# Routing in three phases inside the attention, second choices ranked from the top of an expert's rows, and another order of an attention's first steps

## What is computed

```python
probs = jax.nn.softmax(logits, axis=-1)
top1 = jnp.argmax(probs, axis=-1)
top2 = jnp.argmax(jnp.where(m1 > 0, -jnp.inf, logits), axis=-1)
loc1 = jnp.cumsum(m1, axis=0) - 1.0
loc2 = jnp.cumsum(m2, axis=0) - 1.0 + m1.sum(axis=0, keepdims=True)
m1 = m1 * (loc1 < C); m2 = m2 * (loc2 < C)
h = jax.nn.gelu(jnp.einsum('ecd,edf->ecf', xin, fc1_w) + fc1_b[:, None, :])
eout = jnp.einsum('ecf,efd->ecd', h, fc2_w) + fc2_b[:, None, :]
```

## Time and profile before

| | us |
|---|---|
| median of 3 runs (lowest, highest) | 2134.05 (2132.18, 2135.73) |
| the profiled execution | 2132.52 |
| its span, first to last instruction | 2130.4 |
| PE busy | 1588.8 |
| DVE busy | 1344.6 |
| POOL busy | 1074.2 |
| ACT busy | 944.5 |

### The profile page before, as it was taken

The page is one execution under the profiler, slowest core; times in us unless marked ns, Lnnn a source line. Parts: engine busy times, 40 slices in busy tenths (PEclk is TensorE's granted clock), DMA queues, the critical chain, the costliest instruction groups (busy, mean ns, idle before and its releaser), DMA issues. The chain is left out here.

```text
span 2130.4 us, 44441 instructions
## 1 busy us (share of the span) xinstructions
PE 1588.8 (75%) x16560; PEld 899.4 (42%) x16560; DVE 1344.6 (63%) x3121; ACT 944.5 (44%) x2000; POOL 1074.2 (50%) x1761
## 2 busy tenths in 40 slices
PE   3345888873459899972788389999999999826872
PEld 3242333332435555541334145555555555513431
DVE  8628877826298877738322488777777777473214
ACT  1112666641217567640222146666666666602221
POOL 2144757421438576420777347346456674305773
PEclk9985899965859999985888679999999999957996
DMA  6142223201423233300343333323233233002435
GB/s 207 39 138 79 82 82 84 80 22 40 139 82 112 70 95 92 87 17 25 82 90 93 99 102 91 86 78 99 77 85 92 82 103 86 28 25 61 97 81 145
DMA packets 227411, 178.66 MB, mean 84 GB/s; under 512 B 33479, under 2 KB 216143, under 8 KB 226816
## 3 DMA queue, kind: packets, MB, share of 16 engines
q1 hardware_dynamic: 211776, 155.26, 25.7%
q0 software_dynamic: 10240, 17.96, 4.2%
q10 hardware_dynamic: 5184, 2.63, 0.4%
HBM read 104.34 MB, written 72.35 MB: 83 GB/s over the span
## 5 line engine op out<-in xcount | busy, mean ns | idle before, releaser
L701 DVE TENSOR_REDUCE mx<-PS 128x2 f32<-128x512 f32 (+3 forms) x1408 | 780.5, 610 | 218.4 <-PE PS L386 166.6
L560 ACT ACTIVATE pt<-PS 128x512 f32<-128x512 f32 (+2 forms) x1408 | 657.9, 539 | 316.4 <-PE PS L386 241.2
L402 PE MATMUL PS<-ka,qa 52*128 52x256 bf16 (+3 forms) x2048 | 486.4, 308 | 57.1 <-DVE mx L701 47.4
L511 PE MATMUL PS<-qa,ka 55*128 55x512 bf16 (+3 forms) x1792 | 468.2, 320 | 34.9 <-DMA qa<-nm 28.4
L456 PE MATMUL PS<-pt,vs 128*32 128x512 f32 (+3 forms) x3584 | 348.7, 482 | 0.0
L1244 POOL DMA_INDIRECT pt<-xn_rows,idx x160 | 165.6, 1035 | 340.3 <-DVE idx L1179 292.8
L386 PE MATMUL PS<-mask_q,identh 64*128 64x64 bf16 x3072 | 316.3, 193 | 0.0
L386 PE MATMUL PS<-mask_k,identh 64*128 64x64 bf16 x3072 | 309.3, 190 | 0.0
L511 PEld LDWEIGHTS PS<-qa,ka 55*128 55x128 bf16 x1792 | 166.5, 94 | 262.4 <-issue 135.9
L386 PEld LDWEIGHTS PS<-mask_q,identh 64*128 64x128 bf16 x3072 | 260.6, 98 | 31.5 <-issue 7.8
L386 PEld LDWEIGHTS PS<-mask_k,identh 64*128 64x128 bf16 x3072 | 251.4, 96 | 47.9 <-issue 2.2
(11 more groups left out here) (223 smaller groups left out, 2287.0 us busy)
## 6 DMA issues: line engine op xcount, KB each, us to landing
pt<-in_f_w SPq DMA_DIRECT2D x96, 256.0 KB, 3.3
q_parts<-parts SPq DMA_DIRECT2D x192, 128.0 KB, 2.4
qa<-q_parts SPq DMA_DIRECT2D x256, 96.0 KB, 2.3
k_parts<-parts SPq DMA_DIRECT2D x144, 128.0 KB, 2.4
ka<-k_parts SPq DMA_DIRECT2D x192, 96.0 KB, 2.4
xn_rows<-xn SPq DMA_DIRECT2D x32, 256.0 KB, 2.4
xn<-y_rows SPq DMA_DIRECT2D x32, 256.0 KB, 4.7
hid<-y_rows SPq DMA_DIRECT2D x32, 256.0 KB, 5.3
```

Source lines behind the costliest of these rows:

```text
L402: mm = pe.matmul(PS[:, bank, i * n:(i + 1) * n], k.qa[rows, b % 2, g, h // 2, qb * P:(qb + 1) * P], k.ka[rows, b % 2, g, h // 2, 0:n], sta ...
L511: mm = pe.matmul(PS[:, bank, i * n:(i + 1) * n], k.ka[rows, b % 2, g, h // 2, kb * P:(kb + 1) * P], k.qa[rows, b % 2, g, h // 2, q0:S], st ...
L560: nc.scalar.activation(k.pt[:, u % 2, at[c]:at[c] + len(heads) * n], PS[:, SC_BANK + c % RING, 0:len(heads) * n], ACT.Exp, scale=SCORE_SCA ...
L701: nc.vector.tensor_reduce(out, PS[:, MX_BANK + t % RING, 0:len(heads) * n] .rearrange("p (h n) -> p h n", n=n), AX.X, ALU.max).then_inc(s. ...
```

## The change

**Routing.** `Routing`, `choose`, `ranks`, `mark`, `mark_high`, `occupants` and `index` take the place of the head of `moe`. The 32 tiles are routed in phases of 20, 8 and 4 tiles (`PHASES`); the very first routing is one phase of 32, in the front block. A phase's `choose` makes both one-hot tables (11 linked steps) and one running sum over all its columns; `ranks` is six matmuls of the phase's columns (and two or more short ones for the counts carried over); `mark` handles both choices in one pass. A second choice's rank is counted from the top end of its expert's rows, so that it doesn't need the total of first choices; the gates take that total in at the end. Phase 0 is chosen in unit U-2 and marked in unit U-1; phase 1 is chosen between `o_T` and `out` of the tail and marked after `front_rows`; phase 2 follows the last logits. Multiplying the high marks goes to POOL (`mark_high`), but for phase 2 of an attention.

**Experts.** What the gates need (`differences`, `shares`, `gates`) stands between the copies of the first experts, and the scaling of the source between those of experts 1 to 8. SP waits for the stores and loads the results of batch 0 before the block ends.

**Ramp.** `enter(2)` goes: POOL adds batches 2 (ahead of unit 0) to 7 (units 1, 2, 5, 6, 9), the DVE makes deviations at units 3, 7 and 11. `norm(1)` follows the key split and the values, and unit 0's maxima follow it at once; batch 1's projections stand between unit 1's maxima. The parts of a side go out in three DMAs, each repeating its source for 3, 2 and 1 rows, each as soon as its part is there. ACT loads the exponential's table first.

```diff
-WRITES = NPROD
+WRITES = 3
...
+class Routing:
...
+def choose(nc, k, chain, r, j):
...
+    over_e = lambda ap: ap.unsqueeze(2).to_broadcast([P, n, E])
+    logits, held, rest = e3(k.logits[:, cols]), e3(k.rw[:, 0:n * E]), e3(k.rw[:, 512:512 + n * E])
+    onehot = [r.onehot(k, j)[:, c].rearrange("p e t -> p t e") for c in range(2)]
+    for c, values in ((0, logits), (1, rest)):
+        top, last = k.rv[:, c, a:b], k.rv[:, 2 + c, a:b]
+        if c == 1:
+            chain.link(nc.vector.scalar_tensor_tensor(rest, onehot[0], MASKED, logits, ALU.mult, ALU.add))
+        chain.link(red(top, values, AX.X, ALU.max))
+        chain.link(tt(held, values, over_e(top), ALU.is_equal))
+        chain.link(tt(held, held, broadcast_rows(r.w.down, n), ALU.mult))
+        chain.link(red(last, held, AX.X, ALU.max))
+        chain.link(tt(onehot[c], held, over_e(last), ALU.is_equal))
+    upto, flat = r.upto(k, j), k.onehot[:, 2 * E * a:2 * E * b]
+    nc.vector.memset(upto[:, 0:1], 0.0)
+    chain.link(nc.vector.tensor_tensor_scan(upto[:, 1:], k.onesf[:, 0:1].to_broadcast([P, 2 * E * n]), flat, 0.0,
+                                            ALU.mult, ALU.add))
+    before, upto_end = r.ends(k, j)
+    ins = tt(k.carry[:, j, 0:2 * E], upto_end, before, ALU.subtract)
+    if 0 < j < len(r.phases) - 1:
+        chain.link(ins)
+        ins = tt(k.carry[:, j, 0:2 * E], k.carry[:, j, 0:2 * E], k.carry[:, j - 1, 0:2 * E], ALU.add)
+    ins.then_inc(s.choice_ready.h, 1)
+    chain.eng.wait_ge(*s.choice_ready.at(j + 1))
...
+def ranks(pe, k, r, j):
...
+    pe.wait_ge(*s.choice_ready.at(j + 1))
+    spread = lambda ap: ap.unsqueeze(2).to_broadcast([P, E, n])
+    by_e = lambda ap: ap.rearrange("p (e t) -> p e t", e=E)
+    before, upto, onehot = r.ends(k, j)[0], r.upto(k, j)[:, 1:], r.onehot(k, j)
+    for c in range(2):
+        out = PS[:, RANK_BANK + c, 0:n * E]
+        pe.matmul(out, k.onesb[:, :], upto[:, c * E * n:(c + 1) * E * n], start=True, stop=False)
+        pe.matmul(by_e(out), k.minus[:, :], spread(before[:, c * E:(c + 1) * E]), start=False, stop=False)
+        if j:
+            pe.matmul(by_e(out), k.onesb[:, :], spread(k.carry[:, j - 1, c * E:(c + 1) * E]), start=False, stop=False)
+        mm = pe.matmul(by_e(out), k.upper[:, :], onehot[:, c], start=False, stop=True)
+    if j == len(r.phases) - 1:
+        first = max(j - 1, 0)
+        for i in range(first, j + 1):
+            mm = pe.matmul(PS[:, RANK_BANK, 512 - E:512], k.onesb[:, :], k.carry[:, i, 0:E], start=(i == first), stop=(i == j))
+    mm.then_inc(s.rank_full.h, 1)
...
+def mark(nc, k, chain, r, j, alone):
...
+    rank, part, row, tile, last = both(10), both(12), both(14), both(16), both(2)
+    held = k.rw[:, 0:2 * n * E].rearrange("p (c e t) -> p c e t", c=2, e=E)
+    chain.eng.wait_ge(*s.rank_full.at(j + 1))
+    chain.link(tt(held, k.PS[:, RANK_BANK:RANK_BANK + 2, 0:n * E].rearrange("p c (e t) -> p c e t", e=E), r.onehot(k, j),
+                  ALU.mult))
+    chain.link(nc.vector.tensor_reduce(rank, held.rearrange("p c e t -> p c t e"), AX.X, ALU.add))
+    chain.link(nc.vector.tensor_scalar(part, rank, float(P), None, ALU.is_ge))
+    for m in range(2, ST):
+        chain.link(stt(part, rank, float(m * P), part, ALU.is_ge, ALU.add))
+    chain.link(stt(row, part, -float(P), rank, ALU.mult, ALU.add))
+    stt(tile[:, 0, :], last[:, 0, :], -float(ST), part[:, 0, :], ALU.mult, ALU.add)
+    chain.link(stt(tile[:, 1, :], last[:, 1, :], -float(ST), part[:, 1, :], ALU.mult, ALU.subtract))
+    marks = [r.marks(k, c, a, b) for c in range(2)]
+    for c, (low, high) in enumerate(marks):
+        last_high = tt(high, broadcast_rows(r.w.tile_names[c], n), tile[:, c, :].unsqueeze(2).to_broadcast([P, n, r.tiles]),
+                       ALU.is_equal)
+    chain.link(last_high)
+    for c, (low, high) in enumerate(marks):
+        last_low = nc.vector.tensor_scalar(low, high, k.lane[:, 0:1], None, ALU.mult)
+    if alone:
+        chain.link(last_low)
+        for c, (low, high) in enumerate(marks):
+            last_high = tt(high, high, k.row_high[:, a:b].unsqueeze(2).to_broadcast([P, n, r.tiles]), ALU.mult)
+        last_high.then_inc(s.high_ready.h, 1)
+    for c in range(2):
+        last_row = tt(k.at_rank[:, c, a * P:b * P].rearrange("p (t r) -> p t r", r=P), broadcast_rows(k.row_names[c], n),
+                      row[:, c, :].unsqueeze(2).to_broadcast([P, n, P]), ALU.is_equal)
+    last_row.then_inc(s.marks_ready.h, 1)
+    chain.eng.wait_ge(*s.marks_ready.at(j + 1))
...
+def occupants(pe, k, r, j):
+    s, (a, b) = k.sig, r.phases[j]
+    pe.wait_ge(*s.marks_ready.at(j + 1))
+    pe.wait_ge(*s.high_ready.at(j + 1))
+    for c in range(2):
+        for t in range(a, b):
+            mm = pe.matmul(k.PS[:, INV_BANK, c * 2 * r.tiles:(c + 1) * 2 * r.tiles], k.at_rank[:, c, t * P:(t + 1) * P],
+                           k.in_tile[c][:, 2 * r.tiles * t:2 * r.tiles * (t + 1)], start=(c == 0 and t == 0), stop=(c == 1 and t == NT - 1))
+    if j == len(r.phases) - 1:
+        mm.then_inc(s.inv_full.h, 1)
...
+def index(nc, k, chain, r):
...
+    chain.eng.wait_ge(*s.inv_full.at(1))
+    inv = k.PS[:, INV_BANK, 0:4 * n].rearrange("p (c a n) -> p c a n", c=2, a=2)
+    found = k.rw[:, 0:2 * n].rearrange("p (c n) -> p c n", c=2)
+    token, empty = k.rw[:, 512:512 + n], k.rw[:, 768:768 + n]
+    chain.link(nc.vector.tensor_copy(found, inv[:, :, 1, :]))
+    chain.link(nc.vector.tensor_tensor(found, inv[:, :, 0, :], found, ALU.add))
+    chain.link(stt(token, found[:, 0, :], 0.0, found[:, 1, :], ALU.is_equal, ALU.mult))
+    chain.link(nc.vector.tensor_tensor(token, token, found[:, 0, :], ALU.add))
+    ts(k.idx[:, 0, 0:n], token, -1.0, float(T), ALU.min, ALU.add)
+    chain.link(ts(empty, found[:, 0, :], 0.0, float(T), ALU.is_equal, ALU.mult))
+    stt(k.idx[:, 1, 0:n], empty, float(T), token, ALU.add, ALU.add).then_inc(s.idx_ready.h, 1)
+    chain.link(ts(k.before[:, 0:r.E], k.PS[:, RANK_BANK, 512 - r.E:512], float(r.w.counted), None, ALU.min))
 def front_counts(k):
...
+    LATE_ENTRY = {-1: 2, 1: 3, 2: 4, 5: 5, 6: 6, 9: 7}
+    LATE_ROOT = {3: 3, 7: 4, 11: 5}
     entered = lambda b: sum(first <= b for first, n in ENTRY_GROUPS)
...
         if u in LATE_ENTRY:
             events += [("late0", LATE_ENTRY[u])]
-        if u - 1 in LATE_ENTRY:
+        if u - 1 in LATE_ENTRY and u:
             events += [("late2", LATE_ENTRY[u - 1])]
-        if u == max(LATE_ENTRY) + 2:
-            events += [("late_root", 3)]
+        if u in LATE_ROOT:
+            events += [("late_root", LATE_ROOT[u])]
...
+        if u == U - 2:
+            events += [("choose", 0)]
+        if u == U - 1:
+            events += [("ranks", 0), ("mark", 0)]
...
+            for name in ENTRY + ("v",):
+                project(name, 0)
             pe.wait_ge(*s.steps_landed.at(32))
-            for u in range(2):
-                for t in range(NMX):
-                    max_tile(u, t)
-                if u == 0:
-                    max_transpose(u)
+            for t in range(NMX):
+                max_tile(0, t)
+            max_transpose(0)
+            for t in range(NMX):
+                max_tile(1, t)
+                if t in (2, 5):
+                    project(ENTRY[t // 3], 1)
...
-            for name in ("ctx_T", "out", "f_T", "f_l"):
+            for name in ("ctx_T", "out"):
                 tail(name, NB - 1)
+            ranks(pe, k, r, 1)
+            occupants(pe, k, r, 0)
+            for name in ("f_T", "f_l"):
+                tail(name, NB - 1)
+            occupants(pe, k, r, 1)
+            ranks(pe, k, r, 2)
+            occupants(pe, k, r, 2)
...
-                for name in ENTRY:
-                    copy(name, b)
+            nc.scalar.activation(k.spare[:, 0:1], k.ident[:, 0:1], ACT.Exp)
+            for name in ENTRY:
+                copy(name, 0)
             copy("nm", 0)
+            for name in ENTRY:
+                copy(name, 1)
             for u in range(U):
                 for name, n in order(u):
...
             split_first_keys()
             value_rows(0)
-            if conv:
-                convolve(1)
-            enter(2)
-            for u in range(2):
-                for t in range(NMX):
-                    max_tile(u, t)
+            norm(1)
+            for t in range(NMX):
+                max_tile(0, t)
+            for t in range(NMX):
+                max_tile(1, t)
+                if t == 5 and conv:
+                    convolve(1)
+            entry(2, 2)
+            entry_deviations(2)
...
+                    elif name == "choose":
+                        dve.wait_ge(*s.gl_free.at(PHASES[0][1] // TB))
+                        choose(nc, k, route, r, 0)
+                    elif name == "mark":
+                        dve.wait_ge(*s.pv_done.at(U - 1))
+                        mark(nc, k, route, r, 0, False)
             tail("o_T", U // 2 - 1)
+            dve.wait_ge(*s.gl_free.at(PHASES[1][1] // TB))
```

(55 more changed lines are left out.)

337 lines of the change are left out of this document (159 added, 178 removed).

## The result

The changed kernel takes 2060.35 us (median of 4 runs, 2055.78 to 2064.37) beside 2133.11 us before (4 runs, 2121.93 to 2135.73): a ratio of 0.967, 95% interval 0.963 to 0.971. The forecast was 2032 us, 2010 to 2058. The direction was right; 73 us came in place of 102, and the median lies 2 us above the range. The profiled execution has a span of 2059.4 us and a time of 2061.11.

What follows compares the result with a forecast made beforehand. It took linked DVE routing chains as the bound for 167 us, then ramp waits, with PE bounding units and POOL's DMAs experts. 8.6 + 16.6 + 44 - 5.7 + 32.5 + 2.4 + 4 = 102.4 us gave 2032 us, range 2010 to 2058.

Steps and rivals of the forecast that it cites:

- Routing in the attentions: Logits to first fetch inside attentions: phases partly hidden beside units, 16.6 us gained with 8 experts, 22 twice with 16.
- The rule on the running sum: DVE running sums in routing: built-in one goes at half throughput, by which the sums would cost 1.5 us more in all.
- First routing: One-phase routing of 8 experts in the front block: first fetch at 84.5 against 93.2, 8.6 us gained.
- the step that said it is hidden: choose(0) in unit U-2: 320 columns, 6.9 us, hidden because no row maxima are left there.
- the step that failed: Attention units: three smaller late_roots replace one that stops PE 4.8 us, and POOL adds one more batch; 4 us gained.
- The prediction's own first paragraph: What bounds the kernel: a linked DVE step costs 0.155 us plus columns/960, and 0.035 to the next.
- The bounds 0 and 9: Limits set on the gain in the attention units, in us, of which 4 was taken.
- Ramps: Attention's block start to first score: earlier result loads, split writes and maxima gain 32.5 us over three ramps.
- The keys' path: Last ramp: batch 0 as before until its keys at 1207.0, then key loads at 1217.8 against 1227.81.
- Experts: Expert stages: gates ahead of result(0) delays the first delivery and so all, 5.7 us lost together.
- the first (ramps give half): Rival: first score waits for something after the maxima, ramps give 16 in place of 32.5, 2048 us; chance 0.12.
- The second (POOL in full): Rival: tail handovers pay POOL's products in full, 5 us more per 16-expert tail, 4 in others, 2050; chance 0.12.

Runs made afterwards that it cites:

- The held `choose(0)`: Changed kernel with choose(0) held until POOL's front rows are written, ranks(0) and mark(0) later: unit U-2 18.4 and 16.9 us, last score to fetch 45.3 and 45.1.
- the high products on the DVE: Changed kernel with the high products of phases 0 and 1 on the DVE, none on POOL: last score to first fetch 43.5 and 43.8 us.
- the spread roots: Changed kernel with three late roots issued one step behind each maximum tile: second attention's body 330.3 us, 18.3 less, of which 3.0 are unit 0's.

## Why the prediction was right and wrong

*Routing in the attentions*: right in its mechanism. Forecast 16.6, 22 and 22; measured 18.8, 22.1 and 22.2 from the last score on (19.7, 19.0 and 21.3 if the last unit, which now holds `ranks(0)`, is counted in), with `o_T` 5.6 us later, `mark(0)` 13.1 (12.8). That the last two came to 0.2 is in part luck. Two sizes inside were too small: POOL beside `choose(1)` 3.2 instead of 2.5, and `choose(1)` on its own 5.7 instead of 4.5. The stretch from `out` to the logits made up for them: 7.9 us where 9.0 was measured before and 9.6 forecast. PE, busy there with `occupants`, was granted a higher clock (last column but two; the kernel before, then the changed one), and its transposes and gate products, 1.12 and 1.86 us before, took 0.66 and 1.24:

```profile
1869.60:1878.60 9.00, 2.98 (x12) 2.50 (x12) 4.36 (x21) 0.99 (x2) 0.00 (x0) 0.50 0.10 29
1833.20:1841.10 7.90, 6.49 (x60) 6.00 (x60) 7.28 (x31) 1.00 (x2) 0.00 (x0) 0.72 0.12 35
```

The 1.2 us in `choose(1)` are the two one-hot writes, 0.9, and the running sum, 0.3. In its strided bf16 order a one-hot write of 128 columns takes 0.72 us where f32 in row order takes 0.29. The Trainium skill has this in "SBUF — State Buffer", "Door 1: The DMA port swizzle", in its remark on cachelines: an access that goes to a new 16-byte line each time pays for it, and these elements lie eight bf16, 16 bytes, apart. The trace agrees. The same instruction with 64 columns, in phase 1 of the first attention (16 bytes apart) and in phase 2 of the last (8 bytes apart):

```profile
458.60 0.44 DVE L313 TENSOR_TENSOR onehot<-rw,rv 128x64 bf16<-128x64 f32 x1
1848.39 0.30 DVE L313 TENSOR_TENSOR onehot<-rw,rv 128x64 bf16<-128x64 f32 x1
```

The Trainium skill has two hits to a line as enough there for full speed; here two elements to a line still took longer than 64 f32 columns in row order, 0.22 us. Whether that is the stride or the bf16 output, no run tells. The rule on the running sum (cited in the prediction) holds: 256 columns took 0.69 us, where a product of 512 does.

*First routing*: 6.6 of 8.6. `mark` took 13.2 (13.3); `choose` took 8.3 and not 6.0, by the same strided writes and sums.

*`choose(0)` beside the units*: the step that said it is hidden, since the DVE idles, looked at one engine. It priced POOL beside the DVE in the tail and not here, where the DVE's steps stretch POOL's rows, for which PE waits: unit U-2 grew by 5.7 and 4.4 us, and 4.2 of each is this wait. It also took 6.9 us for a phase that measures 9.9. The held `choose(0)` removed the wait in unit U-2 and lost as much behind it, so no run shows a place for it that costs nothing.

*Units*: the step that failed, and with it the prediction. It read the earlier trace rows rightly (a root stops PE 4.8 us and makes its unit 7 longer) and then wrote that three smaller ones take its place for a gain of 4. The prediction's own first paragraph has the reason against it: a step costs a fixed part, and a root of 4 or 16 columns is all fixed part. By its steps alone three roots cost three times the one; measured, 26.0 us in three units against 7.0 in one, +19.0, as they also stand where POOL splits (6.9 us each, against 5.6 for the old one). Unit 0's +5.7 (+2.8 in the runs with the longer ramp) is the third batch's root, for which the prediction took 3 in the ramp. In all the units gave +37.6 where -4 was put, 41.6 us off: 24.7 of it are roots, 10.1 the two units U-2 with `choose(0)`. The bounds 0 and 9 were both on the side of gain, so no part of the range stood for units that grow. That the median missed the range by only 2 us is luck: the ramps' 13 us more than forecast hid part of the error.

*Ramps*: 45.5 instead of 32.5, a term mis-sized on the side of gain. In the last one the first sum came 5.1 us after the last delivery, before the change 12.7 (1200.55 in the earlier trace rows less 1187.9); the forecast had 7.2 from the block's start against 9.1 and so took 1.9 us. It left out the block change between the last delivery and the first load, 3.5 us before, and that the loads behind the constant rows were slow to issue as well: 1.64 and 2.66 us for the first two, where they take 0.37 and 0.51 now. Run alone, this order is worth 6.2 to 8.3 us per ramp. The keys' path was overrated in turn: from the first transposes to the first maxima 15.6 us against 20.8, 5.2 saved and not 8. The 1207.0 that the prediction gives for batch 0's keys is where its first transposes start in the kernel before; ACT writes the keys out only by 1214.5 there. The 17.5 us from there to the first score were forecast as 17.7.

*Experts*: +10.6 instead of +5.7, all of it with 8 experts; `gates` explains 0.7 to 3 of each, and the rest stays open.

*The rivals*: the first (ramps give half) went the other way. The second (POOL in full) is what happens in the tail, where the rule of the Trainium skill's "SBUF — State Buffer", "Who interferes with whom", holds to the row: a step with two SBUF inputs beside a POOL step that reads SBUF lasts until that one ends, and the reduction after it doesn't. It forecast 5 us more per tail; the high products on the DVE show POOL's whole price as 3.2 and 1.5, 1.0 more than the sum had. None of the rivals had the units growing: what they lacked was a case in which the new linked steps stop PE.

## What to carry to other kernels

Splitting a chain of small linked steps into several chains multiplies it: count steps, not columns. If such a chain must stand in a stream that another engine lives on, put one step behind each element of the stream; that was worth 16 us here and needed no new buffer. And before calling a place on an idle engine free, look at who works beside it there and who waits for that one: 9.9 us of work on an idle DVE made PE wait 4.2 us longer, by way of POOL. When such a place is then changed, add up every stage behind it: the 4.2 us that one unit gave back were gone again by the first fetch.

## What the runs showed of the hardware

After PE had paused for 4 to 6 us, its granted clock was 0.50 in the 6 to 8 us that followed, although it was busy throughout: by an estimate from these rows, a pause costs half of that stretch on top of itself. With the spread roots the clock was 0.92 from 662 to 668 us, 0.69 from 668 to 672 and 1.00 from 672 to 688.

It goes the other way too: with `occupants` in PE's gaps between `out` and the last logits its clock was 0.72 in place of 0.50, and the stretch took 7.9 us in place of 9.0.

POOL suffers as much as the DVE: beside `choose(0)` its 4-column product L133 took 1.01 us in place of 0.20, and eight row steps 8.49 in place of 6.26.

The 16-expert stage of the changed kernel and its variants took 173 to 175 us in the first profile and on one chip of the experiments, and 189 to 198 on the three others, with most units of the attentions equal to 0.1 us in all of them. Why is open.
